# Decoder layer on one core: the keys, the output projection and the second norm in earlier slots of a step

## The reference, cut to what matters

```
x  = layernorm(x + scan(x, A, B) W' + b)          # h[l] = A h[l-1] + B x[l]
q, k, v = projections of x (q) and of ctx (k, v); rotary on q and k
p  = softmax over keys with |query - key| <= 50, 16 heads of 16 channels
x  = layernorm(x + (p v) Wo' + bo)
router: probs = softmax over tokens of silu(x w1r) w2r; top 64 tokens of each of 16 experts
x  = layernorm(sum over experts of weight * (silu(x w1) * (x w2)) w3, added at the chosen tokens)
```

## Time and profile before

| | us |
|---|---|
| three timed runs: lowest, median, highest | 1069.51, 1070.06, 1073.17 |
| the profiled execution | 1072.09 |
| its span, first to last instruction | 1070.3 |
| TensorE busy (matmuls) | 991.9 (93%) |
| VectorE busy | 729.6 (68%) |
| GpSimd busy | 672.7 (63%) |
| ScalarE busy | 591.3 (55%) |

### The profile page before, as it was taken

One profiled execution on the slowest core, in us unless ns is written; L12 is line 12 of the kernel. 1 busy time (PEld: TensorE's weight loads), 2 busy tenths in 40 slices (PEclk: granted clock), 3 DMA queues, 4 the chain that ended last, 5 costly groups with the idle time before them and its releaser, 6 DMA issues.

```text
span 1070.3 us, 21269 instructions
## 1 busy us (share of the span) xinstructions
PE 991.9 (93%) x6436; PEld 845.4 (79%) x6436; DVE 729.6 (68%) x2168; ACT 591.3 (55%) x1234; POOL 672.7 (63%) x784
## 2 busy tenths in 40 slices
PE   4799999999989998879999999999999999999990
PEld 3578778777877877658898888888888888888880
DVE  4678888888877798757554787565556756765633
ACT  1155565556565555456656555555555556555642
POOL 5556666666666565267757665776666767666543
PEclk8899999999999999899999999999999999999995
DMA  6344344433333332525676666666676666666636
GB/s 191 84 103 98 100 106 103 103 99 102 102 101 97 85 81 70 182 94 168 156 223 124 160 141 168 136 158 152 160 218 158 141 155 149 147 155 143 184 54 176
DMA packets 114918, 142.56 MB, mean 133 GB/s; under 512 B 15104, under 2 KB 88064, under 8 KB 114688
## 3 DMA queue, kind: packets, MB, share of 16 engines
q1 hardware_dynamic: 86432, 105.56, 34.2%
q0 software_dynamic: 24576, 33.57, 18.1%
q10 hardware_dynamic: 3808, 2.22, 0.7%
HBM read 90.70 MB, written 29.36 MB: 112 GB/s over the span
## 4 chain that ended last, share of the span: by engine, by line
PE 52%; ACT 1%; DMA 1%; POOL 1%; issue 1%; DVE 0%; ACTq 0%; POOLq 0%; SPq 0%
PE gate_bank L1349 16%; PE attn L1349 16%; PE value_bank L1349 16%; PE turn_bank L1359 2%; DMA last<-acc_rows 0%; ACT last L1590 0%; DMA acc_rows<-y,slots_now 0%; PE attn L1432 0%; PE attn L1406 0%; POOL acc_rows L1294 0%; DVE stats L1627 0%; DVE hidden L1620 0%; ACTq L1594 0%; ACT w_hi L1482 0%; POOL rstd L167 0%
## 5 line engine op out<-in xcount | busy, mean ns | idle before, releaser
L1294 POOL DMA_INDIRECT acc_rows<-y,slots_now x128 | 205.6, 1607 | 137.4 <-issue 73.4
L787 ACT ACTIVATE probsT<-scoreT 128x356 f32<-128x356 f32 x256 | 117.7, 468 | 137.6 <-PE scoreT L618 113.3
L945 DVE CUSTOM_DVE_ANT_0 scored<-score,band 128x178 f32<-128x178 f32 x512 | 149.9, 337 | 63.3 <-PE score L589 59.4
L1620 DVE TENSOR_TENSOR hidden<-gate,value_bank 128x512 f32<-128x512 f32 x128 | 87.9, 687 | 152.7 <-ACT gate L1495 152.6
L1495 ACT ACTIVATE gate<-gate_bank 128x512 f32<-128x512 f32 x128 | 76.6, 598 | 188.3 <-PE value_bank L1349 188.3
L1349 PE MATMUL attn<-w_hi,h_hi 128*128 128x256 f32 x512 | 146.1, 285 | 0.2
L1349 PE MATMUL attn<-w_hi,h_lo 128*128 128x256 f32 x512 | 143.3, 280 | 0.0
L1349 PE MATMUL attn<-w_lo,h_hi 128*128 128x256 f32 x512 | 143.3, 280 | 0.0
L589 PE MATMUL score<-k_stack,q_stack 96*128 96x178 f32 x512 | 123.8, 325 | 7.2 <-DVE nmax L945 4.2
L589 PEld LDWEIGHTS score<-k_stack,q_stack 96*128 96x128 f32 x512 | 88.9, 194 | 37.1 <-DVE nmax L945 17.3
L618 PE MATMUL scoreT<-q_stack,k_stack 97*128 97x356 f32 x256 | 116.5, 456 | 0.0
(11 more groups left out here) (214 smaller groups left out, 2374.9 us busy)
## 6 DMA issues: line engine op xcount, KB each, us to landing
arena<-in_w SPq DMA_DIRECT2D x96, 512.0 KB, 4.0
k_stack<-high_k SPq DMA_DIRECT2D x128, 64.0 KB, 2.2
q_stack<-high_q SPq DMA_DIRECT2D x128, 64.0 KB, 2.3
arena<-in_xT SPq DMA_DIRECT2D x16, 256.0 KB, 2.9
arena<-in_x SPq DMA_DIRECT2D x16, 256.0 KB, 3.1
arena<-in_cT SPq DMA_DIRECT2D x16, 256.0 KB, 3.7
k_stack<-low_k SPq DMA_DIRECT2D x64, 64.0 KB, 2.3
q_stack<-low_q SPq DMA_DIRECT2D x64, 64.0 KB, 2.2
```

The source lines that it names most:

```text
L787: nc.scalar.activation(probsT[g % 2][:, u % HG, :, :].rearrange("p a s -> p (a s)"), scoreT[u % 2][:, 0:2 * SPAN], ACT.Exp, scale=1.0 / DH ...
L945: op = nc.vector.tensor_tensor_reduce(scored[t % 2][:, q, :], score[t % 2][:, q * SPAN:(q + 1) * SPAN], band[:, q, :], -1.0, BIG, ALU.add, ...
L1294: nc.gpsimd.indirect_dma_start(dram["acc"][c], bass.IndirectOffsetOnAxis(ap=now[:, m:m + 1], axis=0), y[m][:], None, compute_op=ALU.add).t ...
L1620: nc.vector.tensor_tensor(hidden[f % 2][:], gate[f % 2][:], value_bank[f % 2][:], ALU.mult).then_inc(hidden_ready, 1)
```

## The change

It moves work between slots of a step and between places of each engine's queue. Nothing is computed otherwise.

- `NORMAL`: both halves of O in slot 2 (from 4 and 7), statistics in slot 3 (8), estimate in 4 (9), normalise in 7 (11), OX in 9 (13), the copy to `x2T` in 10 (14), R in 14 (15). The copy to `r1` stays in 15, now ahead of that slot's exponentials.
- K in slot 0 (from 1), behind X; its rotation on VectorE in slot 2 (3).
- OX uses the bank of K, O, V and R, between O and V.
- VectorE adds the first odd group in slot 4 (3).
- ScalarE evicts K in slot 1 (2) and Q in slot 4, both ahead of the slot's copy of maxima and exponentials, copies X in slot 0 (1), and makes the keys' high part in slot 4 (5).
- GpSimd makes the keys' low part right after the keys' rotation, and refines the second norm's deviation ahead of the queries' rotation.
- SiLU in slot 2 of step 10 (slot 9), the router's second product in slot 15 of step 10, after R (slot 13 of step 11), the logits' copy and maximum in the same slot on VectorE, the router's exponential in slot 4 of step 11 (slot 1 of 12), scaling in slot 8 of step 11 (slot 2 of 12), the eight rounds in slots 14 and 0 of steps 11 to 15, the picks' turn in slot 11 of step 15 (10).

```diff
@@ -255,7 +255,7 @@
...
 
-        ORDER = (("X", "Q", "U", "Y", "OX"), ("K", "O", "V", "R"))
+        ORDER = (("X", "Q", "U", "Y"), ("K", "O", "OX", "V", "R"))
         ready, freed = ({n: sem(f"{what}_{n}") for names in ORDER for n in names} for what in ("ready", "freed"))
...
@@ -315,11 +315,14 @@
...
 
-        NORMAL = {"O": (4, 7), "statistics": 8, "estimate": 9, "normalise": 11, "OX": 13, "x2T": 14, "R": 15, "r1": 15}
+        NORMAL = {"O": (2, 2), "statistics": 3, "estimate": 4, "normalise": 7, "OX": 9, "x2T": 10, "R": 14, "r1": 15}
         DRAIN = {"O": (1, 2), "statistics": 2, "estimate": 3, "normalise": 5, "OX": 6, "x2T": 7, "R": 8, "r1": 9}
...
             return DRAIN if it.fixed and it.i >= NB else NORMAL
+
+        def odd_at(it):
+            return 3 if it.fixed and it.i >= NB else 4
 
...
@@ -519,19 +522,16 @@
...
                         rotate(it, 0)
+                        lower(it, 0)
                     cosine(it, 1)
+                if there(it, "O"):
+                    inverse_deviation(it, "O")
                 if there(it, "Q"):
                     rotate(it, 1)
-                    if not hoisted(it):
-                        lower(it, 0)
                     lower(it, 1)
                 drain = it.fixed and it.i >= NB
-                if drain and there(it, "O"):
-                    inverse_deviation(it, "O")
                 if behind:
                     inverse_sums(it, -2)
-                if there(it, "O") and not drain:
-                    inverse_deviation(it, "O")
                 if there(it, "Y"):
...
@@ -671,28 +671,30 @@
...
                         gather(it, t)
-                    if t == 1 and there(it, "K") and not hoisted(it):
-                        keys(it)
                     if t == 6 and it.fixed and it.i == -2:
...
                         transposed(it, "X", x1[(it.r + 1) % 4])
+                    if t == 0 and there(it, "K") and not hoisted(it):
+                        if it.fixed and it.i == 11:
+                            pe.wait_ge(logits_kept, 1)
+                        keys(it)
                     if t == 3 and there(it, "Q"):
...
                         project(it, "Q", wq, x1T)
-                    if t in slot(it)["O"] and there(it, "O"):
-                        n = slot(it)["O"].index(t)
...
+                    for n in range(TT):
+                        if t == slot(it)["O"][n] and there(it, "O"):
...
                     if t == 5 and there(it, "U"):
...
@@ -704,15 +706,7 @@
...
                         transposed(it, "OX", x2cur)
-                    if only(it, 11, t, 13):
-                        pe.wait_ge(rw2_set, 1)
-                        pe.wait_ge(silu_done, 1)
-                        pe.wait_ge(freed["V"], uses(it, "V"))
-                        for c in range(GB):
-                            mm = nc.tensor.matmul(bank("R")[:, 0:S], rw2_placed[:, c, :], r1[:, c * S:(c + 1) * S],
-                                                  start=(c == 0), stop=(c == GB - 1))
-                        mm.then_inc(logits_ready, 1)
-                    if only(it, NB - 1, t, 10):
+                    if only(it, NB - 1, t, 11):
                         pe.wait_ge(route.picked, 1)
...
@@ -730,8 +724,6 @@
...
                     if t == slot(it)["R"] and there(it, "R"):
-                        if it.fixed and it.i == 11:
-                            pe.wait_ge(logits_kept, 1)
                         if it.fixed and it.i == NB - 1:
...
@@ -740,6 +732,14 @@
...
                         mm.then_inc(ready["R"], 1)
+                    if only(it, 10, t, 15):
+                        pe.wait_ge(rw2_set, 1)
+                        pe.wait_ge(silu_done, 1)
+                        pe.wait_ge(freed["R"], uses(it, "R") + FREED_EARLY["R"])
+                        for c in range(GB):
+                            mm = nc.tensor.matmul(bank("R")[:, 0:S], rw2_placed[:, c, :], r1[:, c * S:(c + 1) * S],
+                                                  start=(c == 0), stop=(c == GB - 1))
+                        mm.then_inc(logits_ready, 1)
 
...
@@ -857,24 +857,27 @@
...
                 for t in range(NH):
+                    if t == slot(it)["r1"] and there(it, "R"):
+                        act.wait_ge(ready["R"], uses(it, "R"))
+                        nc.scalar.copy(r1[:, bass.ds(it.lin(S, -2 * S), S)], bank("R")[:, 0:S]).then_inc(freed["R"], 1)
+                    if t == 1 and there(it, "K") and not hoisted(it):
+                        biased(it, 0)
+                    if t == 4 and there(it, "Q"):
+                        biased(it, 1)
                     if t in (1, 5, 9, 13):
...
                     exponentials(it, t)
-                    if t == 2 and there(it, "K") and not hoisted(it):
-                        biased(it, 0)
+                    if t == 0 and there(it, "X"):
+                        columns(it, "X", x1T)
                     if it.fixed and it.i == -2 and t == 7:
                         biased(FIRST_KEYS, 0)
-                    if t == 1 and there(it, "X"):
-                        columns(it, "X", x1T)
                     if t in (7, 15):
...
                         invert_sums(it, -2 if t == first else -1)
-                    if t == 4 and there(it, "Q"):
-                        biased(it, 1)
-                    if t == 5 and there(it, "K") and not hoisted(it):
+                    if t == 4 and there(it, "K") and not hoisted(it):
                         heighten(it, 0)
...
@@ -882,12 +885,12 @@
...
                         heighten(it, 1)
-                    if only(it, 10, t, 9):
+                    if only(it, 10, t, 2):
                         act.wait_ge(freed["R"], GB + FREED_EARLY["R"])
...
                         act.preload_act_table_set("natural_log_exp_and_others")
-                    if only(it, 12, t, 1):
+                    if only(it, 11, t, 4):
                         act.wait_ge(route.nmax_ready, 1)
...
@@ -900,9 +903,6 @@
...
                         estimate(it, "Y")
-                    if t == slot(it)["r1"] and there(it, "R"):
-                        act.wait_ge(ready["R"], uses(it, "R"))
-                        nc.scalar.copy(r1[:, bass.ds(it.lin(S, -2 * S), S)], bank("R")[:, 0:S]).then_inc(freed["R"], 1)
 
...
@@ -985,9 +985,9 @@
...
                     maxima(it, t)
-                    if t in (3, 11) and has(it, group(t, 15)) and not only(it, NB, t, 11):
-
-                        p = group(t, 15) // 2
+                    if t in (odd_at(it), 11) and has(it, group(11 if t == 11 else 3, 15)) and not only(it, NB, t, 11):
+
+                        p = group(11 if t == 11 else 3, 15) // 2
                         b = p % 2
...
@@ -998,7 +998,7 @@
...
                         nc.vector.stream_shuffle(sums[b][:], mixed[b][:], swap).then_inc(sums_ready, 1)
-                    if t == 3 and there(it, "K") and not hoisted(it):
+                    if t == 2 and there(it, "K") and not hoisted(it):
                         rotated(it, 0)
...
@@ -1042,14 +1042,14 @@
...
                         normalise(it, "Y", x1[(it.r + 2) % 4], x1_ready)
-                    if only(it, 11, t, 14):
+                    if only(it, 10, t, 15):
                         dve.wait_ge(logits_ready, 1)
...
                         find_maximum(dve, route, route.p[:])
-                    if only(it, 12, t, 2):
+                    if only(it, 11, t, 8):
                         scale_probabilities(dve, route)
-                    for n, (i, at) in enumerate(((12, 7), (12, 14), (13, 1), (13, 14), (14, 1), (14, 14), (15, 1), (15, 4))):
+                    for n, (i, at) in enumerate(((11, 14), (12, 0), (12, 14), (13, 0), (13, 14), (14, 0), (14, 14), (15, 0))):
                         if only(it, i, t, at):
...
```

More of the change, by code:

```diff
@@ L685, in step @@
                         project(it, "Q", wq, x1T)
-                    if t in slot(it)["O"] and there(it, "O"):
-                        n = slot(it)["O"].index(t)
-                        if n == 0:
-                            begin(it, "O")
-                            pe.wait_ge(attnT_ready, it.lin(NPAIR, -NPAIR))
-                        for g in range(NPAIR):
-                            mm = nc.tensor.matmul(bank("O")[:, n * D:(n + 1) * D], attnT[it.r % 2][:, g, n * P:(n + 1) * P],
-                                                  wo[:, g, :], start=(g == 0), stop=(g == NPAIR - 1))
-                        if n == TT - 1:
-                            mm.then_inc(ready["O"], 1)
+                    for n in range(TT):
+                        if t == slot(it)["O"][n] and there(it, "O"):
+                            if n == 0:
+                                begin(it, "O")
+                                pe.wait_ge(attnT_ready, it.lin(NPAIR, -NPAIR))
+                            for g in range(NPAIR):
+                                mm = nc.tensor.matmul(bank("O")[:, n * D:(n + 1) * D], attnT[it.r % 2][:, g, n * P:(n + 1) * P],
```

(3 more changed lines are left out.)

## The result

| | before | after |
|---|---|---|
| time, median of the runs (us) | 1070.84 | 1082.86 (1081.49 to 1083.95) |
| profiled execution, span | 1072.09, 1070.3 | 1081.49, 1079.7 |
| ratio, with 95% interval | | 1.011 (1.0092 to 1.0128) |

The change made the kernel 12.0 us slower where I had forecast 3. Between the two profiled executions it is 9.4 us.

The account below looks back on a forecast made before the run. TensorE's queue plus the x2 turn's hole bound steps 2 to 9; -1.17 -0.22 +1.35 +0.46 +0.10 made 26.67 us a step. Eight steps +4.2, others -1.8 -0.4 -1.4 +2.2: +2.8, so 1073 us, range 1062 to 1081.

Parts of the forecast that it names:

- steady step: One pass of sixteen slots in steps 2 to 9: from 26.15 to 26.67 us, +0.5 each.
- steps 2 to 9: The eight loop steps, each taken at the new step time: +4.2 us together.
- steps 10 and 11: SiLU and router product move, the product no longer waits: 58.41 to 56.6 us, -1.8.
- steps 14 to 16: Last mixing steps: step 14 -1.4 us, half of it clock; steps 15 and 16 +2.2, range 0 to +3.
- The turn's 1.17: TensorE's wait for the second norm at the turn of x2 in slot 13: removed, -1.17 us a step.
- The waits of slot 8: TensorE newly waits for VectorE at slot 8's scores and the mixer's second product: +1.35 us a step, restarts included.
- Slot 14: Its gather waits for ScalarE's copy of slot 13's maxima, formerly covered by the hole: +0.46 us a step.
- TensorE's own queue: Same products in other slots, with score, output projection and weight-load terms: -0.22 us a step.
- q: Queries' term in VectorE's chain to slot 8: about 1.83 us, between 1.37 alone and 2.16 beside the whole cosine.
- Rival A: Queries' product meets GpSimd's whole cosine, normalise slowed too: 12 steps at +0.47, 1078.6 us; chance 0.24.
- C: Hole only moves: late normalise holds slot 8's maxima and the turn, 1 us more a step, 1085; chance 0.06.
- B: VectorE's chain mostly covered, slot 14's wait met by slack: step 25.6 to 25.9, 1062 us; chance 0.25.

Follow-up runs that it names:

- e5: Kernel after, with GpSimd running the queries' cosine product before the keys' low part: 1074.55 us, ratio 1.0034.
- e1: Kernel after, with the second norm alone put back in its old slots (statistics 8, estimate 9, normalise 11, turn 13): 1090.29 us.
- e10: e1 with the output projection back in slots 4 and 7 as well: 1068.95 us, ratio 0.9979.
- e6: Kernel after, with VectorE's addition moved from slot 4 to the end of slot 2: 1072.13 us.
- e9: Kernel before, with the addition alone moved from slot 3 to slot 4: 1070.80 us.
- e15: Kernel after, with step 15's output projection in slots 4 and 5 and its norm behind it: 1079.77 us, ratio 1.0074.
- e13: e11 with step 15's output projection in slots 4 and 5 and its norm behind it: 1059.01 us, ratio 0.9876.
- e7: e6 with GpSimd's queries' cosine product before the keys' low part as well: 1068.91 us, ratio 0.9968.
- e11: e7 with GpSimd's keys' low part behind the second norm's inverse deviation: 1063.42 us, ratio 0.9922.

## Why the prediction was wrong

**The step that failed** is the sum outside the steady step. It took the eight loop steps as alike, booked SiLU's move into slot 2 as free and put steps 14 to 16 at +0.8. From +2.8 forecast to +9.4 in the profiles 6.6 us are missing: 1.5 in steps 2 to 9, 1.5 in steps 10 and 11, 0.3 in steps 12 and 13, 2.5 in steps 14 to 16, 0.7 in steps 0 and 1 and 0.1 elsewhere. Each is taken up below.

**The steady step was right, in its size by luck.** Forecast 26.67, measured 26.64. The turn's 1.17 is gone, and x2 was there 1.4 us before TensorE came to slot 9 (1.5 forecast). The waits of slot 8 are 1.30, with the two restarts (1.61 for 1.54 at the mixer's product, 0.30 for 0.20 at the scores) 1.47, where I had 1.35. Slot 14: 0.46 forecast, 0.27 (0.18 at the scores, 0.09 at the gather). Slot 2: 0.10 forecast, none. What is left is TensorE's own queue: 26.64 - (26.07 - 1.17 + 1.47 + 0.27) = 0.00, where I had -0.22. From their starts to those of the products behind them the sixteen pairs of score products of a step take 5.17 before and 5.00 after, where I had 5.32 and 4.83, and the whole output projection costs 0.28 more than its halves, not 0.20; the 0.07 for weight loads no row shows. So slot 8 and the own queue cost 0.34 more than forecast, slots 14 and 2 0.29 less, and the base of 26.15, which held the loop's turn, was 0.08 too high. The queries' sine product met part of the cosine, as walked: q was 1.69 (286.49 to 288.18) for 1.83. e5 shows that the cosine was a term, 0.31 a step where the forecast's two values of q differ by 0.45.

In its cause the sum was loose. I had written that VectorE's list grows "because the second norm's statistics move into slot 3 and the odd gather's addition into slot 4". e1 shows the statistics at 0.2 of 1.85 us: in a chain that runs over two engines VectorE stops for slot 4's scores anyway. The length of the chain was right all the same, since VectorE is busy or waiting there for about as long. The first half of that paragraph (the projection's halves leave TensorE's stretch) was the part that decided, with the addition: e10 and e6 each take the waits away.

**Steps 2 to 9:** +4.2 forecast, +5.7 measured (5.5 from turn of x1 to turn of x1). Seven steps at 0.57 are 4.0; the step at the loop's turn grew by 1.5 (26.68 to 28.19). The sum took it as one of eight alike; why it grew with the change is not shown.

**Steps 10 and 11:** -1.8 forecast, -0.3. SiLU's stop (0.84 and 0.46 by the starts, in slot 5) does cover slot 8's wait in step 10, of which 0.15 is left, but it costs as much itself; I had booked it as free. Slot 14's scores wait in both steps (0.33, 0.47).

**Steps 14 to 16:** -1.4 and +2.2, so +0.8 forecast; -0.5 and +3.8, so +3.3 measured in the windows. This is the term that was mis-sized most. I had stops of 1.6 in step 15 (one of 1.52 came), but no lower clock behind them: 0.81 granted in steps 15 and 16, 0.88 before. As e9's profile differs from that of the kernel before by as much, the size of this term is rough; by the medians the projection's place in step 15 is worth 3.1 (e15) to 4.4 us (e13).

**Steps 0 and 1:** within 0.2 forecast, +0.2 and +0.5 measured, in single profiles.

The other 2.6 us of the 12.0 are not in the profiles: after, the profiled execution lay 1.4 below its median, before 1.2 above. I took the median of three runs, 2.0 below the profiled one, as base; with the later runs of that kernel at 1071.3 to 1072.1 this alone made the forecast some 1 us low.

**The chances.** Rival A (the full collision, 1078.6) was nearest by number, not by way: the sine product stayed at 0.98. C was wrong, the turn never waited in the steady steps. The first half of B's condition (a queries' term of 1.37 or less) is e5, at 26.33; B's step of 25.6 to 25.9 needed the addition's move too (e6, e7).

## What to carry to other kernels

Before moving work to fill a hole of the leading engine, ask what that work hid where it stood: the projection's work in slots 4 and 7 hid VectorE, in slot 2 it hides nothing. In a chain over two engines, work that fits between two hand-overs is free up to the next hand-over (statistics, 0.2 of 1.85 us), while work with no stop behind it shows up at the next wait (the addition: 1.15 of 1.40 us at slot 8, and 0.74 of the step, as new stops took the rest). So sum from hand-over to hand-over, not over the list. And price the steps that aren't like the others (the loop's turn, the last ones) by themselves: what the forecast missed lay there.

## What the runs showed of the hardware

The sine product (VectorE) against the large product of GpSimd beside it, in e7, e11 and, above, in the kernel after and e1. Timeline of e7:

```profile
256.22 1.28 POOL L471 TENSOR_TENSOR low_k<-raw_k,high_k 128x512 fp32r<-128x512 f32 x1
...
256.71 1.34 DVE L983 TENSOR_TENSOR arena<-arena,sin 128x512 f32<-128x512 f32 x1
```

and of e11:

```profile
252.24 0.69 DVE L983 TENSOR_TENSOR arena<-arena,sin 128x512 f32<-128x512 f32 x1
252.33 0.65 POOL L170 TENSOR_TENSOR newton_O<-newton_O,rstd_O 128x2 f32<-128x2 f32 x1
```

GpSimd's products end at 287.71, 267.28 and 257.50, the sine products begun beside them at 288.25, 267.83 and 258.05: 0.54 to 0.55 later each time, however early they had begun. That is a queue for the whole instruction, not a slowdown by a share. The Trainium skill states (SBUF — State Buffer, Who interferes with whom) that a VectorE instruction with two SBUF inputs contends with a GpSimd one that reads SBUF, and that the contention is an exclusive lock; the trace agrees. It holds the other way as well: in e11 a GpSimd product of two elements a partition, 0.20 us elsewhere, took 0.65 and ended 0.05 after the sine product. And it isn't only products of two tensors: the first half of e6's normalise (rows above), which reads one large tensor and two numbers for each partition, took 1.25 beside GpSimd's product (259.58 to 260.83) where it takes 0.42 after the change, and ended 0.15 after it.
